# A two-layer graph kernel: attended half of the gate products in three f16 passes, products taken mask by mask, and a reordered first stage

## The chip, the cores and the metric

The kernel runs on one core of a Trainium2 chip. The metric is the device time of one execution in microseconds (us). The engines are TensorE (PE, with its weight loads shown as PEld), VectorE (DVE), ScalarE (ACT), GpSimd (POOL) and SyncE (SP), which issues most of the DMAs. Each engine works through its own list in order, and they meet only at semaphores.

## What is computed

There are 8192 nodes with 128 features each, and an adjacency matrix of 8192 x 8192 zeros and ones.

```python
h = relu(layernorm(x))
# first layer: graph attention, then a gated (GRU) update
Wh = h @ W;  src = Wh @ a[:F];  dst = Wh @ a[F:]
e = leaky_relu(src + dst.T, 0.2)
att = softmax(where(adj > 0, e, NEG_INF), axis=1)
h_prime = att @ Wh
gi = h_prime @ w_ih.T + b_ih          # the "attended half" of the gates
gh = h @ w_hh.T + b_hh
r = sigmoid(i_r + h_r);  z = sigmoid(i_z + h_z);  n = tanh(i_n + r * h_n)
x = x + (1 - z) * n + z * h
# second layer: plain aggregation
h = relu(layernorm(x))
x = x + adj @ (h @ W1.T + b1)
```

## The kernel before, in words

The file also has a path for any adjacency; it runs only where a check at the end asks for it, and takes no part here. The work is in `binary_adjacency`.

**First stage (0 to about 107 us).** Layernorm of all rows, their transposes, `h @ W` with its two attention columns (`column` and `features` on ACT, `weighted` on PE), and stores of h in two layouts. SP issues the stores in a loop over k = 0..15, and among them two loads of adjacency chunks (X, 2 MB each). Then come some small DVE operations on the attention columns and tables of f16 numbers (TB): `exp` factors times `Wh`, split into a high and a low half (`table_product`, `table_high`, `table_low`).

**Attention stage (107 to about 1139 us).** The rows are taken in 32 blocks of 256, called slots, g = 0..31. A slot has four chunks c = 0..3 of 2048 columns. For each chunk DVE and ACT make a mask "src + dst is positive" (`compare`, L669, 7 tiles on DVE; `sign_mask`, L468, 9 tiles on ACT), DVE turns the adjacency chunk into bytes (`ones_of`, L618), and combines both into two masks (`combine`: AND at L677, mask 1, and XOR at L681, mask 2). PE multiplies both masks with the tables: 64 matmuls of 259 columns for a chunk (`products`, L893), accumulating in four PSUM banks A[t][m], t being the half of the 256 rows and m the mask. ACT also counts the ones of each chunk (L477).

When the slot is done, its sums go through a tail that runs beside the next slots. With q = g - 1, in slot g: ACT copies the four banks (`evacuate`, L489), DVE forms `h_prime` in hp (`attended`, L686 to L702, placed after DVE's chunk c = 1), PE transposes it after its chunk 0 (L903, semaphore g_a), ACT copies the transpose to hpT (`attended_columns`, L503, semaphore g_1, placed in ACT's chunk 3), and PE computes the gates after its chunk 1 (`gates`, L916 to L919), preceded by a wait on g_1 and by the transposes of the normed rows of g - 2 (`normed`, L925). The sigmoids, tanh, update, second layernorm and the product with W1 (`projected`, L936) follow one or two slots later.

The chunk numbers of the engines are not the same time. DVE makes the masks of a slot while PE multiplies those of the slot before or the chunks just made: DVE's `attended` for slot g - 1 stands after DVE's chunk 1 of slot g, and it can start only when PE has ended slot g - 1.

**Second stage (1139 us to the end).** The mask bytes, stored by the first layer, are read again and multiplied with the projected rows (`span` and `rest`, L975).

The order on each engine is written out by hand in `slot`, `after` and `each_row_block` (slots 0 to 3 and the last two are written out, the rest is a loop over pairs). The lines that matter most here:

```python
def after(g, u, k, c):                 # PE, behind each chunk's products
    if c == 0 and in_range(g, 1):
        attended(g - 1)
    if c == 1:
        if in_range(g, 1):
            pe.wait_ge(g_1, g)
        if in_range(g, 2):
            normed(g - 2)
        if in_range(g, 1):
            gates(g - 1, 1 - u, k if u else k - 1)
```

Of the kernel before, what the change touches and what calls it, by code (L numbers as in the profile page):

```python
# [35 lines left out]
WNORM = 2.0  # L36
STEEP = 2.0 ** 60
# [30 lines left out]
def binary_adjacency(nc, sem, redo, xb, adjb, w, wt, a, wiht, whht, b_ih, b_hh, w1t, b1, out):  # L68
    ctx = ExitStack()
    with ctx:  # L70
# [18 lines left out]
        hpT = sb("hpT", [P, RW])  # L89
# [5 lines left out]
        wihT = sb("wihT", [P, 3 * F])  # L95
# [9 lines left out]
        rden = sb("rden", [P, 2])  # L105
# [12 lines left out]
        den = sb("den", [P, NT])  # L118
# [27 lines left out]
        dmb = rz[:, :, :].rearrange("p t f -> p (t f)")[:, 0:P]  # L146
# [18 lines left out]
        A = [[ps(f"A{t}{m}") for m in range(2)] for t in range(2)]  # L165
# [5 lines left out]
        WB = [A[0][0], A[0][1], A[1][0], A[1][1]]  # L171
        TP = [TG, GQ]
        PH2 = [A[0][0], A[0][1], A[1][0], A[1][1]]
# [12 lines left out]
        t_sc = k_w = sem("t_sc")  # L186

# [7 lines left out]
        e_t0, e_ev = sem("e_t0"), [sem(f"e_ev{t}") for t in range(2)]  # L195
# [40 lines left out]
        with nc.Block() as block:  # L236
            @block.sync
            def _(sp):
# [8 lines left out]
                for k in range(16):  # L247
# [105 lines left out]
            def _(pool):  # L353
# [21 lines left out]
                nc.gpsimd.tensor_tensor(brow[0:2, :], brow[0:2, :], bhid, ALU.add).then_inc(p_bias, 1)  # L375
                src = [brow] + bres
                for k in range(3):
                    pool.wait_ge(p_bias, 2 * k + 1)
                    nc.gpsimd.tensor_copy(bpart[k], src[k]).then_inc(p_bias, 1)
                    if k < 2:  # L380
                        pool.wait_ge(p_bias, 2 * k + 2)
                        nc.gpsimd.tensor_tensor(bres[k], src[k], bpart[k], ALU.subtract).then_inc(p_bias, 1)
                for q in range(4, 8):
                    deviation(q)
                pool.wait_ge(b_in, 112)
                nc.gpsimd.memset(TB[:, :, :, 2 * TW:2 * TW + 2], 1.0).then_inc(p_one, 1)

                def slot(g, u, k):
                    if in_range(g, 2):
                        q = g - 2  # L390
                        pool.wait_ge(d_ve, q + 1)
# [7 lines left out]
            def _(act):  # L399
# [4 lines left out]
                act.dma_start(wihT[:, :], wiht).then_inc(wt_in, 16)  # L404
# [8 lines left out]
                def features(k):  # L413
                    for b in range(2):
                        act.wait_ge(p_wh, 2 * k + b + 1)
                        t = k * 4 + b * 2
                        nc.scalar.activation(
                            WG[:, t:t + 2, 0:F + 2],
                            WB[(2 * k + b) % 4][:, 0:2 * (F + 2)].rearrange("p (t f) -> p t f", f=F + 2),
                            ACT.Copy).then_inc(p_ev, 1)  # L420
# [33 lines left out]
                def sign_mask(g, u, k, c):  # L454
# [8 lines left out]
                    for jj in range(first_on_act(g), JC):  # L463
                        if isinstance(g, int) and g == 0 and jj == JC // 2:
# [16 lines left out]
                def evacuate(q):  # L481
                    for t in range(2):
                        if t == 0:
                            act.wait_ge(e_t0, q + 1)
# [3 lines left out]
                        for m in range(2):  # L488
                            ins = nc.scalar.activation(AE[:, 2 * t + m, 0:2 * TW + 1], A[t][m][:, 0:2 * TW + 1], ACT.Copy)  # L489
                        ins.then_inc(e_ev[t], 1)  # L490

                def gate_sigmoids(q):
                    act.wait_ge(g_b, q + 1)
                    wait(act, d_x1, q)
                    nc.scalar.activation(rz[:, :, :], GP3[:, :, 0:2 * F], ACT.Sigmoid).then_inc(g_2, 1)

                def candidate(q):
                    act.wait_ge(d_tmp, q + 1)
                    nc.scalar.activation(nn[:, :, :], tmp[:, :, :], ACT.Tanh).then_inc(g_3, 1)
# [64 lines left out]
            def _(dve):  # L564
# [56 lines left out]
                ones_of(0, 0, 0, 0)  # L621
                dve.wait_ge(p_ev, 32)
# [17 lines left out]
                nc.vector.tensor_copy(srow, GP[0:NT, P:2 * P]).then_inc(p_sq, 1)  # L640

# [41 lines left out]
                def attended(q):  # L683
                    for t in range(2):
                        dve.wait_ge(e_ev[t], q + 1)
                    nc.vector.tensor_tensor(AE[:, :, 0:TW], AE[:, :, 0:TW], AE[:, :, TW:2 * TW], ALU.add).then_inc(d_sum, 1)  # L686
                    nc.vector.tensor_tensor(cn[:, bass.ts(q, 2)],
                                            AE[:, 0:4:2, 2 * TW:2 * TW + 1].rearrange("p t f -> p (t f)"),
                                            AE[:, 1:4:2, 2 * TW:2 * TW + 1].rearrange("p t f -> p (t f)"), ALU.add)
                    dve.wait_ge(d_sum, q + 1)  # L690
                    for t in range(2):
                        ins = nc.vector.scalar_tensor_tensor(nm[:, t, :], AE[:, 2 * t + 1, 0:TW],
                                                             ct[:, bass.ds(q * 2 + t, 1)], AE[:, 2 * t, 0:TW], ALU.mult,
# [4 lines left out]
                    nc.vector.reciprocal(rden[:, :], total).then_inc(d_rec, 1)  # L698
                    nc.vector.tensor_copy(den[:, bass.ts(q, 2)], total)
                    dve.wait_ge(d_rec, q + 1)  # L700
                    for t in range(2):
                        ins = nc.vector.tensor_scalar(hp[:, t * F:(t + 1) * F], nm[:, t, 0:F], rden[:, t:t + 1], None,  # L702
                                                      ALU.mult)
                    ins.then_inc(d_hp, 1)

# [7 lines left out]
                def updated(q, u, n):  # L713
# [23 lines left out]
                    dve.wait_ge(d_mv, q + 1)  # L737
                    nc.vector.tensor_scalar(ve[:, :], mv[:, :, 1:2].rearrange("p t k -> p (t k)"), EPS, None,  # L738
                                            ALU.add).then_inc(d_ve, 1)
# [14 lines left out]
                def slot(g, u, k):  # L754
                    main = in_range(g, 0)
                    first = isinstance(g, int) and g == 0
                    for c in range(CS):
                        if main:
# [12 lines left out]
                            combine(g, c)  # L771
                        if c == 0 and in_range(g, 2):
# [913 lines left out]
```

## Time and profile before

| what | value |
|---|---|
| median of 3 runs | 1602.78 us (1601.82 to 1603.23) |
| the profiled execution's own time | 1601.98 us |
| its span, first to last instruction | 1600.4 us |
| mean granted TensorE clock | 0.985 of 2.4 GHz |
| busy: PE | 1534.7 us (96%) |
| busy: DVE | 1125.8 us (70%), 193.6 us of each 200 us in the attention stage |
| busy: ACT | 1071.0 us (67%), 192.6 us of each 200 us in the attention stage |
| busy: POOL | 40.5 us (3%) |

The time lies 1.6 us above the span. The busy shares are means over stages: DVE and ACT are nearly full until 1107 us and nearly idle behind it, PE is full from 132 us on. In the timelines a matmul's duration includes its way through the array; the rate of the engine is read from start to start. One slot takes 32.76 us in the attention stage.

### The profile page before, as it was taken

What the parts mean: (1) busy time and instruction counts of PE and PEld (TensorE: products, weight loads), DVE (VectorE), ACT (ScalarE), POOL (GpSimd) and SP (SyncE); (2) the same over time, 40 slices, a digit from 0 to 9 for tenths busy, and PEclk for the clock granted to TensorE, in tenths of its full rate; (3) what the DMA queues carried; (4) which work ended last, traced back from release to release, by engine and by line L of the source; (5) the groups of instructions that cost most, each with busy time, mean ns of one, the idle gap of its engine ahead of it and who ended that gap; (6) DMA issues with size and microseconds to landing.
All of it is one profiled execution on the core that took longest, in us unless ns stands there. A gap on an engine that the chain in (4) does not pass through costs nothing.

```text
span 1600.4 us, 34919 instructions
## 1 busy us (share of the span) xinstructions
PE 1534.7 (96%) x13260; PEld 1333.3 (83%) x13260; DVE 1125.8 (70%) x2274; ACT 1071.0 (67%) x1820; POOL 40.5 (3%) x59
## 2 busy tenths in 40 slices
PE   6369999999999999999999999999999999999998
PEld 5257888888888888888888888888888888888887
DVE  7898999999999999999999999999250000000001
ACT  6689999999999999999999999999121000000000
POOL 4000000000000000000000000000000000000000
PEclk9779999999999999999999999999999999999999
DMA  8759899999999999999999998997468444444430
GB/s 306 292 217 358 332 342 340 345 339 337 342 342 344 332 342 343 342 343 332 340 341 334 346 344 333 346 345 265 191 242 334 177 176 163 156 161 170 177 126 15
DMA packets 79954, 454.15 MB, mean 284 GB/s; under 512 B 9176, under 2 KB 38434, under 8 KB 58914
## 3 DMA queue, kind: packets, MB, share of 16 engines
q1 hardware_dynamic: 78322, 444.54, 74.9%
q10 hardware_dynamic: 1584, 8.98, 1.4%
q8 instruction: 28, 0.46, 0.1%
q14 instruction: 20, 0.16, 0.0%
HBM read 369.57 MB, written 83.92 MB: 283 GB/s over the span
## 4 chain that ended last, share of the span: by engine, by line
PE 93%; DVE 4%; ACT 1%; issue 1%; DMA 1%; SPq 0%; DVEq 0%
PE A L893 56%; PE A L975 28%; PE GP L917 3%; PE GP L918 2%; PE GQ L936 1%; PE GP L919 1%; PE GP L916 1%; ACT M L468 1%; DVE Y L618 1%; DVE JK L568 1%; DMA X<-in_adjb_dram 1%; DVE M L585 0%; PE TG L903 0%; PE TG L925 0%; DVE M L681 0%
## 5 line engine op out<-in xcount | busy, mean ns | idle before, releaser
L893 PE MATMUL A<-TB,M 128*128 128x259 f16 x8192 | 942.4, 275 | 37.8 <-DVE M L681 31.9
L893 PEld LDWEIGHTS A<-TB,M 128*128 128x128 fp8e4 x8192 | 798.2, 97 | 165.4 <-issue 39.0
L468 ACT ACTIVATE M<-SB,dsteep 128x256 fp8e4<-128x256 f32 x1180 | 484.5, 504 | 0.0
L477 ACT ACTIVATE JK<-X 128x4096 uint8<-128x4096 uint32 x124 | 448.4, 3616 | 0.0
L618 DVE TENSOR_SCALAR Y<-X 128x4096 fp8e4<-128x4096 f32 x128 | 293.1, 2290 | 9.9 <-DMA X<-in_adjb_dram 9.6
L796 DVE SCALAR_TENSOR_TENSOR hp<-A,R 128x256 f32<-128x256 f32 x32 | 13.6, 425 | 367.5 <-PE A L975 348.2
L669 DVE TENSOR_SCALAR M<-SB,nd 128x256 fp8e4<-128x256 f32 x868 | 238.4, 349 | 0.0
L975 PE MATMUL A<-WG,X 128*128 128x256 f16 x2048 | 225.7, 273 | 0.0
L975 PE MATMUL A<-WG,TB 128*128 128x256 f16 x2048 | 225.2, 273 | 0.0
L975 PEld LDWEIGHTS A<-WG,TB 128*128 128x128 fp8e4 x2048 | 200.4, 98 | 23.2
L975 PEld LDWEIGHTS A<-WG,X 128*128 128x128 fp8e4 x2048 | 200.4, 98 | 23.1
L681 DVE TENSOR_TENSOR M<-Y,M 128x1024 uint32<-128x1024 uint32 x128 | 156.8, 1225 | 4.5
L677 DVE TENSOR_TENSOR M<-M,Y 128x1024 uint32<-128x1024 uint32 x128 | 156.3, 1221 | 0.5 <-issue 0.4
L489 ACT ACTIVATE AE<-A 128x259 f32<-128x259 f32 x128 | 42.0, 385 | 43.4 <-PE A L893 43.4
L917 PE MATMUL GP<-wihT,hpT 128*128 128x384 f32 x128 | 51.7, 486 | 0.0
L392 POOL TENSOR_TENSOR rstd<-ve,half 128x2 f32<-128x2 f32 x32 | 22.7, 709 | 1108.6 <-DVE ve L738 1108.6
L686 DVE TENSOR_TENSOR AE<-AE 128x516 f32<-128x516 f32 x32 | 22.4, 700 | 22.9 <-ACT AE L489 22.8
L918 PEld LDWEIGHTS GP<-whhT,R 128*128 128x128 f32 x128 | 24.3, 190 | 17.0
L918 PE MATMUL GP<-whhT,R 128*128 128x256 f32 x128 | 38.1, 379 | 0.0
L919 PEld LDWEIGHTS GP<-whhT,R 128*128 128x128 f32 x128 | 24.3, 190 | 3.3
L555 ACT ACTIVATE JK<-M 128x4096 uint8<-128x4096 uint32 x4 | 14.5, 3617 | 18.6 <-DMA M<-in_adjb_dram 18.6
L917 PEld LDWEIGHTS GP<-wihT,hpT 128*128 128x128 f32 x128 | 24.3, 190 | 2.4
(132 smaller groups left out, 687.3 us busy)
## 6 DMA issues: line engine op xcount, KB each, us to landing
X<-in_adjb_dram SPq DMA_DIRECT2D x128, 2048.0 KB, 9.2
mask_bytes<-Y SPq DMA_DIRECT2D x128, 512.0 KB, 4.8
X<-mask_bytes SPq DMA_DIRECT2D x16, 2048.0 KB, 9.3
TB<-mask_bytes SPq DMA_DIRECT2D x16, 2048.0 KB, 9.2
M<-in_adjb_dram ACTq DMA_DIRECT2D x4, 2048.0 KB, 10.6
M<-in_xb_dram SPq DMA_DIRECT2D x8, 512.0 KB, 8.4
h_rows<-M SPq DMA_DIRECT2D x8, 512.0 KB, 3.6
R<-in_xb_dram SPq DMA_DIRECT2D x32, 128.0 KB, 6.7
```

Of the source, the lines that this page charges most:

```text
L468: ins = nc.scalar.activation(rows(mask1(c), jj), SB[u][:, :], ACT.Sigmoid, scale=STEEP, bias=dsteep[:, j:j + 1], saturate=False)
L477: nc.scalar.activation(junk, X[c % 2][:, :].bitcast(u32), ACT.Sign, accum_out=nz[:, bass.ts(g, 1), c:c + 1].rearrange("p g c -> p (g c)")) ...
L489: ins = nc.scalar.activation(AE[:, 2 * t + m, 0:2 * TW + 1], A[t][m][:, 0:2 * TW + 1], ACT.Copy)
L618: nc.vector.tensor_scalar(Y[c % 2][:, :].bitcast(f8), X[c % 2][:, :], 1.0, MARK, ALU.is_equal, ALU.mult, saturate=False).then_inc(c_y, 1)
L669: ins = nc.vector.tensor_scalar(rows(mask1(c), jj), SB[u][:, :], nd[:, j:j + 1], None, ALU.is_ge, saturate=False)
L677: nc.vector.tensor_tensor(mask1(c), mask1(c), Y[c % 2][:, :], ALU.bitwise_and).then_inc(c_m1, 1)
L681: nc.vector.tensor_tensor(mask2(c), Y[c % 2][:, :], mask1(c), ALU.bitwise_xor).then_inc(c_m2, 1)
L893: ins = nc.tensor.matmul(A[t][m][:, 0:2 * TW + 1], rows((mask1, mask2)[m](c), jj)[:, t * P:(t + 1) * P], TB[:, c * JC + jj, m, 0:2 * TW + ...
L917: nc.tensor.matmul(bank[:, 0:3 * F], a_t, wihT[:, :], start=False, stop=False)
L918: nc.tensor.matmul(bank[:, 0:2 * F], h_t, whhT[:, 0:2 * F], start=False, stop=False)
L919: ins = nc.tensor.matmul(bank[:, 3 * F:4 * F], h_t, whhT[:, 2 * F:3 * F], start=False, stop=True)
L975: ins = nc.tensor.matmul(PH2[b][:, d * 2 * F:(d + 1) * 2 * F], YB[b][:, j * RW + d * P:j * RW + (d + 1) * P], GS[:, j, :], start=(d == 0 a ...
```

## The change: what it does

1. **Gate products.** hpT, the transposed `h_prime`, becomes a pair of f16 tiles: ACT writes the high half, and a new DVE operation `attended_low` writes the low half (transpose minus high half). The weights wihT become a pair of f16 tiles too, scaled by 64. PE replaces one f32 matmul of 384 columns by three f16 matmuls (high x high, high x low, low x high). PE's wait on g_1 (ACT's copy) becomes a wait on a_lo (DVE's low half; a_lo is the semaphore t_lo counted on). Biases and whhT are scaled by 64 on POOL, and the sigmoid and tanh scale back.
2. **Products mask by mask.** In each chunk PE takes the 32 matmuls of mask 1 for both halves of the rows, then the 32 of mask 2. The waits for the masks are split likewise.
3. **Merged copies.** The PSUM banks are laid out so that one ACT copy covers the two banks of a mask (`evacuate`) and the four blocks of `features`.
4. **First stage.** The load of the first X is issued at k = 9 instead of 11; DVE's first `ones_of` stands behind the small operations on the attention columns instead of ahead of them; ACT makes its second pair of table halves after 6 mask tiles instead of 8.
5. **Small moves.** The add of epsilon moves from DVE to POOL, a DVE copy (`den`, L699) goes, and the final check gets two more DVE operations.

```diff
-        hpT = sb("hpT", [P, RW])
+        hpT = sb("hpT", [P, 2, RW], f16)
-        wihT = sb("wihT", [P, 3 * F])
+        wihT = sb("wihT", [P, 2, 3 * F], f16)
-        A = [[ps(f"A{t}{m}") for m in range(2)] for t in range(2)]
+        ACC = ps("ACC", 4 * 512)
+        bank = [ACC[:, b * 512:(b + 1) * 512] for b in range(4)]
+        A = [[bank[2 * m + t] for m in range(2)] for t in range(2)]
+        a_lo = t_lo
@@ SP, first stage
-                    if k in (11, 15):
-                        b = k // 4 - 2
+                    if k in (9, 15):
+                        b = k // 15
                         sp.dma_start(X[b][:, :], adjb[b, :, :]).then_inc(c_in[b], 16)
@@ ACT
-                        if isinstance(g, int) and g == 0 and jj == JC // 2:
+                        if isinstance(g, int) and g == 0 and jj == JC // 2 - 2:
                 def evacuate(q):
-                    for t in range(2):
-                        if t == 0:
-                            act.wait_ge(e_t0, q + 1)
+                    for m in range(2):
+                        if m == 0:
+                            act.wait_ge(e_m0, q + 1)
                         else:
                             act.wait_ge(c_pe, (q + 1) * CS)
                         wait(act, d_hp, q)
-                        for m in range(2):
-                            ins = nc.scalar.activation(AE[:, 2 * t + m, 0:2 * TW + 1], A[t][m][:, 0:2 * TW + 1], ACT.Copy)
-                        ins.then_inc(e_ev[t], 1)
+                        nc.scalar.activation(AE[:, 2 * m:2 * m + 2, 0:2 * TW + 1], A3[m][:, :, 0:2 * TW + 1], ACT.Copy).then_inc(
+                            e_ev[m], 1)
-                    nc.scalar.activation(hpT[:, :], TG[:, 0:RW], ACT.Copy).then_inc(g_1, 1)
+                    nc.scalar.activation(hpT[:, 0, :], TG[:, 0:RW], ACT.Copy).then_inc(g_1, 1)
@@ DVE
-                ones_of(0, 0, 0, 0)
-                dve.wait_ge(p_ev, 32)
+                dve.wait_ge(p_ev, 16)
...
+                ones_of(0, 0, 0, 0)
-                    nc.vector.tensor_copy(den[:, bass.ts(q, 2)], total)
+                def attended_low(q):
+                    dve.wait_ge(g_1, q + 1)
+                    nc.vector.tensor_tensor(hpT[:, 1, :], TG[:, 0:RW], hpT[:, 0, :], ALU.subtract).then_inc(a_lo, 1)
...
                             combine(g, c)
+                        if c == 3 and in_range(g, 1):
+                            attended_low(g - 1)
@@ PE
-                def products(g, c, t):
-                    for jj in range(JC):
-                        for m in range(2):
+                def products(g, c, m):
+                    for t in range(2):
+                        for jj in range(JC):
                 def gates(q, u, n):
-                    pe.wait_ge(g_1, q + 1)
+                    pe.wait_ge(a_lo, 16 + q + 1)
...
-                        nc.tensor.matmul(bank[:, 0:3 * F], a_t, wihT[:, :], start=False, stop=False)
+                        for left, part in ((a_t, 0), (a_t, 1), (a_l, 0)):
+                            nc.tensor.matmul(bank[:, 0:3 * F], left, wihT[:, part, :], start=False, stop=False)
                     if c == 1:
                         if in_range(g, 1):
-                            pe.wait_ge(g_1, g)
+                            pe.wait_ge(a_lo, 16 + g)
-                        pe.wait_ge(c_m2, g * CS + c + 1)
-                        for t in range(2):
+                        for m in range(2):
+                            pe.wait_ge((c_m1, c_m2)[m], g * CS + c + 1)
                             if c == 0:
-                                wait(pe, e_ev[t], g)
+                                wait(pe, e_ev[m], g)
```

How the order changes on DVE, in slot 3: the masks of chunks 2 and 3, and what follows them. M is the mask tile, Y the adjacency bytes, h2n the normed rows. Before:

```order
L702 TENSOR_SCALAR hp<-nm,rden 128x128 x2
L669 TENSOR_SCALAR M<-SB,nd 128x256 x7
L618 TENSOR_SCALAR Y<-X 128x4096
L677 TENSOR_TENSOR M<-M,Y 128x1024
L681 TENSOR_TENSOR M<-Y,M 128x1024
L745 TENSOR_SCALAR h2n<-R,mv,rstd 128x128 x2
L751 SCALAR_TENSOR_TENSOR WG<-GQ,WG 128x2x128
L669 TENSOR_SCALAR M<-SB,nd 128x256 x7
L618 TENSOR_SCALAR Y<-X 128x4096
L677 TENSOR_TENSOR M<-M,Y 128x1024
L681 TENSOR_TENSOR M<-Y,M 128x1024
```

The same place on DVE after the change:

```order
L717 TENSOR_SCALAR hp<-nm,rden 128x128 x2
L685 TENSOR_SCALAR M<-SB,nd 128x256 x7
L634 TENSOR_SCALAR Y<-X 128x4096
L693 TENSOR_TENSOR M<-M,Y 128x1024
L697 TENSOR_TENSOR M<-Y,M 128x1024
L761 TENSOR_SCALAR h2n<-R,mv,rstd 128x128 x2
L767 SCALAR_TENSOR_TENSOR WG<-GQ,WG 128x2x128
L685 TENSOR_SCALAR M<-SB,nd 128x256 x7
L634 TENSOR_SCALAR Y<-X 128x4096
L693 TENSOR_TENSOR M<-M,Y 128x1024
L697 TENSOR_TENSOR M<-Y,M 128x1024
L723 TENSOR_TENSOR hpT<-TG,hpT 128x256
```

The new last row is `attended_low`. It stands behind both chunks' masks, two chunks behind the operation that made hp.

On PE, slot 2, from the transposes of hp (L903) to the gates, with the semaphores that an instruction waits for. Before:

```order
L903 MATMUL TG<-ident,hp 128x128
L893 MATMUL A<-TB,M 128x259 [waits c_m2]
L893 MATMUL A<-TB,M 128x259 x63
L925 MATMUL TG<-ident,h2n 128x128 [waits d_h2,g_1]
L925 MATMUL TG<-ident,h2n 128x128
L916 MATMUL GP<-BI,onesb 128x512 [waits d_tmp,g_in1,g_1]
L917 MATMUL GP<-wihT,hpT 128x384
L918 MATMUL GP<-whhT,R 128x256
L919 MATMUL GP<-whhT,R 128x128
```

The same place on PE after the change:

```order
L925 MATMUL TG<-ident,hp 128x128
L915 MATMUL ACC<-TB,M 128x259 [waits c_m1]
L915 MATMUL ACC<-TB,M 128x259 x31
L915 MATMUL ACC<-TB,M 128x259 [waits c_m2]
L915 MATMUL ACC<-TB,M 128x259 x31
L949 MATMUL TG<-ident,h2n 128x128 [waits d_h2,t_lo]
L949 MATMUL TG<-ident,h2n 128x128
L939 MATMUL GP<-BI,onesb 128x512 [waits d_tmp,g_in1,t_lo]
L941 MATMUL GP<-wihT,hpT 128x384 x3
L942 MATMUL GP<-whhT,R 128x256
L943 MATMUL GP<-whhT,R 128x128
```

The gate block stands at the same place. The semaphore it waits for has changed from g_1 (ACT) to t_lo (DVE's L723), and the f32 matmul with wihT is three f16 matmuls.

## Rows read from the trace of the kernel before

**Rows 1.** the page: busy times, and the chain that ended last by engine

```profile
PE 1534.7 (96%) x13260; PEld 1333.3 (83%) x13260; DVE 1125.8 (70%) x2274; ACT 1071.0 (67%) x1820; POOL 40.5 (3%) x59
...
PE 93%; DVE 4%; ACT 1%; issue 1%; DMA 1%; SPq 0%; DVEq 0%
```

**Rows 2.** timeline of PE, 500 to 535 us: start, us, engine, line, operation, count

```profile
509.87 14.48 PE L893 MATMUL A<-TB,M 128*128 128x259 f16 x128
...
524.40 7.32 PE L893 MATMUL A<-TB,M 128*128 128x259 f16 x64
531.56 0.38 PE L925 MATMUL TG<-ident,h2n 128*128 128x128 f32 x2
531.78 0.38 PE L916 MATMUL GP<-BI,onesb 128*128 128x512 bf16 x1
532.00 0.81 PE L917 MATMUL GP<-wihT,hpT 128*128 128x384 f32 x2
532.64 0.59 PE L918 MATMUL GP<-whhT,R 128*128 128x256 f32 x2
...
534.81 0.39 PE L893 MATMUL A<-TB,M 128*128 128x259 f16 x2
```

**Rows 3.** waits, 200 to 1100 us: total, times, longest

```profile
DVE AE L686 <- ACT AE L489: 13.2, 25, 0.7
```

**Rows 4.** timeline of DVE, 500 to 535 us

```profile
507.91 0.42 DVE L711 TENSOR_TENSOR tmp<-tmp,GP 128x256 f32<-128x256 f32 x1
...
517.99 0.70 DVE L686 TENSOR_TENSOR AE<-AE 128x516 f32<-128x516 f32 x1 [0.56 <-ACT AE L489]
...
519.57 0.17 DVE L699 COPY den<-nm 128x2 f32 x1
519.67 0.48 DVE L702 TENSOR_SCALAR hp<-nm,rden 128x128 f32<-128x128 f32 x2
...
529.19 2.29 DVE L618 TENSOR_SCALAR Y<-X 128x4096 fp8e4<-128x4096 f32 x1
531.39 1.22 DVE L677 TENSOR_TENSOR M<-M,Y 128x1024 uint32<-128x1024 uint32 x1
...
533.79 1.40 DVE L669 TENSOR_SCALAR M<-SB,nd 128x256 fp8e4<-128x256 f32 x5
```

**Rows 5.** timeline of ACT, 500 to 535 us

```profile
517.23 0.66 ACT L489 ACTIVATE AE<-A 128x259 f32<-128x259 f32 x2 [1.23 <-PE A L893]
...
528.55 0.37 ACT L503 ACTIVATE hpT<-TG 128x256 f32<-128x256 f32 x1
```

**Rows 6.** timeline of DVE and PE, 75 to 150 us

```profile
78.56 8.94 PE L893 MATMUL A<-TB,M 128*128 128x259 f16 x64 [5.09 <-DVE M L681]
...
106.34 1.23 DVE L681 TENSOR_TENSOR M<-Y,M 128x1024 uint32<-128x1024 uint32 x1
...
107.67 9.72 PE L893 MATMUL A<-TB,M 128*128 128x259 f16 x64 [4.40 <-DVE M L681]
...
138.71 1.92 DVE L669 TENSOR_SCALAR M<-SB,nd 128x256 fp8e4<-128x256 f32 x7
...
139.28 0.38 PE L916 MATMUL GP<-BI,onesb 128*128 128x512 bf16 x1
```

**Rows 7.** PE in two stretches: us, busy (count), granted clock, DMA share, GB/s

```profile
78.00:80.00 2.00, 1.44 (x7) 0.63 1.08 303
118.00:120.00 2.00, 0.00 (x0) 0.87 0.95 352
```

**Rows 8.** timeline of SP, ACT and DVE, first stage

```profile
34.96 0.45 SPq L255 DMA_DIRECT2D X<-in_adjb_dram  x1
...
41.67 0.83 ACT L417 ACTIVATE WG<-A 128x260 f32<-128x260 f32 x2 [0.20 <-PE A L866]
...
44.23 2.29 DVE L618 TENSOR_SCALAR Y<-X 128x4096 fp8e4<-128x4096 f32 x1 [7.18 <-DMA X<-in_adjb_dram]
...
49.20 1.23 DVE L654 TENSOR_TENSOR AE<-WG,bt 128x1032 f32<-128x1032 f32 x1
```

More of the change, by code:

```diff
@@ L36 @@
 WNORM = 2.0
+WSCALE = 64.0
+WMOST = 2.0 ** 28
 STEEP = 2.0 ** 60
@@ L163, in binary_adjacency @@
         x1_d = nc.dram_tensor("x_after_gat", [P, NT, F], f32).ap()
-        A = [[ps(f"A{t}{m}") for m in range(2)] for t in range(2)]
+        ACC = ps("ACC", 4 * 512)
+        bank = [ACC[:, b * 512:(b + 1) * 512] for b in range(4)]
+        A = [[bank[2 * m + t] for m in range(2)] for t in range(2)]
+        A3 = [ACC[:, m * 1024:(m + 1) * 1024].rearrange("p (t f) -> p t f", f=512) for m in range(2)]
         TG = ps("TG")
@@ L194, in binary_adjacency @@
         g_in = [sem(f"g_in{b}") for b in range(2)]
-        e_t0, e_ev = sem("e_t0"), [sem(f"e_ev{t}") for t in range(2)]
+        e_m0, e_ev = sem("e_m0"), [sem(f"e_ev{m}") for m in range(2)]
         d_sum, d_n, d_rec, d_hp = sem("d_sum"), sem("d_n"), sem("d_rec"), sem("d_hp")
@@ L384, in _ @@
                     deviation(q)
+                pool.wait_ge(wt_in, 48)
+                nc.gpsimd.tensor_scalar(wihf, wihf, WSCALE, None, ALU.mult).then_inc(p_bias, 1)
+                nc.gpsimd.tensor_scalar(whhT[:, :], whhT[:, :], WSCALE, None, ALU.mult).then_inc(p_bias, 1)
+                pool.wait_ge(p_bias, 8)
+                nc.gpsimd.tensor_copy(wihT[:, 0, :], wihf).then_inc(p_bias, 1)
+                pool.wait_ge(p_bias, 10)
+                nc.gpsimd.tensor_tensor(wihT[:, 1, :], wihf, wihT[:, 0, :], ALU.subtract).then_inc(p_bias, 1)
                 pool.wait_ge(b_in, 112)
@@ L390, in slot @@
                         q = g - 2
+                        pool.wait_ge(d_mv, q + 1)
+                        nc.gpsimd.tensor_tensor(ve[:, :], mv[:, :, 1:2].rearrange("p t k -> p (t k)"),
+                                                epst[:, 0:1].to_broadcast([P, 2]), ALU.add).then_inc(d_ve, 1)
                         pool.wait_ge(d_ve, q + 1)
@@ L413, in features @@
                 def features(k):
[L414 to L420, printed above, removed]
+                    act.wait_ge(p_wh, k + 1)
+                    nc.scalar.activation(
+                        WG[:, k * 4:k * 4 + 4, 0:F + 2].rearrange("p (b t) f -> p b t f", t=2),
+                        A3[k % 2][:, :, 0:2 * (F + 2)].rearrange("p b (t f) -> p b t f", f=F + 2),
+                        ACT.Copy).then_inc(p_ev, 1)
                 act.wait_ge(p_one, 1)
@@ L860, in weighted @@
                     pe.wait_ge(p_ht, k + 1)
+                    wait(pe, p_ev, k - 1)
                     for b in range(2):
-                        wait(pe, p_ev, 2 * k + b - 3)
                         for d in range(2):
@@ L914, in gates @@
                         bank = GP[:, t * 512:(t + 1) * 512]
-                        a_t, h_t = hpT[:, t * F:(t + 1) * F], HT[u][:, t * F:(t + 1) * F]
+                        a_t, a_l = [hpT[:, part, t * F:(t + 1) * F] for part in range(2)]
+                        h_t = HT[u][:, t * F:(t + 1) * F]
                         nc.tensor.matmul(bank, onesb[:, :], BI[:, 0:4 * F], start=True, stop=False)
-                        nc.tensor.matmul(bank[:, 0:3 * F], a_t, wihT[:, :], start=False, stop=False)
+                        for left, part in ((a_t, 0), (a_t, 1), (a_l, 0)):
+                            nc.tensor.matmul(bank[:, 0:3 * F], left, wihT[:, part, :], start=False, stop=False)
                         nc.tensor.matmul(bank[:, 0:2 * F], h_t, whhT[:, 0:2 * F], start=False, stop=False)
@@ L958, in slot @@
                                 pe.wait_ge(p_one, 3)
[L959 to L960 removed]
+                        for m in range(2):
+                            pe.wait_ge((c_m1, c_m2)[m], g * CS + c + 1)
                             if c == 0:
[L962 removed]
+                                wait(pe, e_ev[m], g)
                             pe.sem_inc(turn, 1)
[L964 to L965 removed]
+                            ins = products(g, c, m)
+                            if m == 1:
                                 ins.then_inc(c_pe, 1)
                             elif c == CS - 1:
[L968 removed]
+                                ins.then_inc(e_m0, 1)
                         after(g, u, k, c)
```

65 lines of the change are left out of this document (33 added, 32 removed).

## The prediction

> **What bounds the kernel now.** I read the page first, then the timelines of one slot in the middle, engine by engine, then the waits, then the first stage and the stretches in which the clock changes. The page says PE: it is busy 96% of the span and 93% of the chain that ended last lies on it [rows 1]. The timeline of PE shows no gap in a slot: 64 matmuls take 7.16 us (524.40 to 531.56), and the transposes and gate products behind them (531.56 to 534.81) and the next matmuls follow start to start [rows 2]. But DVE is not far behind. It waits for PE once in a slot, ahead of `attended` (L686), for only 0.53 us on average (13.2 us over 25 waits) [rows 3]. That wait ties the two engines together. PE ends a slot's products at about 517.03 (the second 64 of the 128 that start at 509.87 begin there a new slot) [rows 2], ACT copies the last banks from 517.23 [rows 5], and DVE starts `attended` at 517.99 [rows 4]. Everything that DVE does behind `attended` is thus fixed in time against the end of a PE slot, however fast PE becomes.
>
> **The new wait, the largest term.** Before, PE's gates waited for ACT's copy, which starts at 528.55 and takes 0.37 us [rows 5]; PE asks for it at 531.56, 2.6 us later [rows 2], so it costs nothing. Now they wait for `attended_low` on DVE. By the order it stands behind the masks of chunk 3, where in the timeline the next slot's `compare` starts: 533.79 [rows 4]. I take off 0.10 us for the copy L699 that goes (519.57 to 519.67) and add the operation itself, 256 elements from PSUM, like L711: 0.42 us [rows 4]. From the end of a DVE operation to PE's first matmul it is 0.10 us (106.34 + 1.23 to 107.67) [rows 6]. So PE goes on at 533.79 - 0.10 + 0.42 + 0.10 = 534.21 instead of 531.56: a gap of 2.65 us. Queued behind the waiting instruction on PE are `normed`, the gates and chunks 2 and 3, and DVE's next `attended` waits for the end of these. The loop closes: end of PE's slot, `attended`, two chunks of masks and the low half on DVE, gates, chunks 2 and 3 on PE. PE's earlier chunks are no part of it, so nothing that is saved there shortens it. Neither ACT nor the DMAs enter: ACT's copy is ready 5 us before DVE comes to it, and ACT and SP gain time in each slot. ACT may now have to wait for its sigmoids, but inside the slack that ACT gains ahead of its last evacuation (it waits 1.23 us there now [rows 5], and gets the 2.65 on top).
>
> **The three f16 passes.** The f32 matmul of 384 columns takes 0.64 us (532.00 to 532.64), the bf16 one of 512 columns 0.22 (531.78 to 532.00) [rows 2]. Three passes of 384 columns at that rate take 3 x 384 x 0.22 / 512 = 0.495 us. Two halves of the rows save 2 x 0.145 = 0.29 us a slot. This lies behind the gap and counts in full. Bounds: nothing (if the added weight loads show) to 0.33 us (if the products come a little under that rate).
>
> **Slot by slot.** Net 2.65 - 0.29 = 2.36 us. It holds in slots 2 to 30, 29 of them: 68.4 us (slot 2 has one DVE operation fewer; I leave that). In slot 1 DVE is early: 138.71 - 0.10 + 0.42 + 0.10 = 139.13, while PE's gates start at 139.28 [rows 6]: no gap, and 0.29 saved. In slot 31 DVE makes no bytes for a next slot, 2.20 us less (529.19 to 531.39 [rows 4]), so the gap is 0.45 and the net +0.16. The gates of slot 31, after the last slot, save 0.29; matmuls of the second stage cover their wait. Sum: 68.4 - 0.29 + 0.16 - 0.29 = 68.0 us.
>
> **The clock.** A gap in PE's work has a second price here. In the gap that begins at 107.67 + 9.72 = 117.39 [rows 6] the mean granted clock of 118 to 120 us is 0.87 [rows 7]; between full and half (2.4 and 1.2 GHz) this means that it fell at about 119.5, 2.1 us after the last matmul. In the gap of 5.09 us ahead of 78.56 it fell only at about 78.5 (0.63 over 78 to 80) [rows 6, 7]. So the delay varies from 2.1 to 5 us, as if against a beat that the kernel doesn't set, and a gap of 2.65 us lies within it. The smallest price on the page of the attention stage is that of the stretch at 78.56: 64 matmuls took 8.94 us against 7.32 at the full clock [rows 2, 6], 1.62 us more. All of PE's work behind the gap is on the loop, so this adds in full. With no fall the price is 0, with one in each of the 29 slots 47 us. The period of the slots has no reason to keep step with such a beat, so I take somewhat over half, 16 falls: 26 us. The Trainium skill ("TensorE: Matmul & The Clock Gate", section "HAM oscillation — how this bites in real kernels") names idle gaps between bursts of matmuls as what brings the low clock back, and counts a gap as short as the one foreseen here among the harmless; by it there would be no fall and the sum would end at 1670 us. The fall 2.1 us into a gap speaks against it.
>
> **Mask by mask.** PE can start a chunk one XOR (1.23 us, L681 [rows 6]) earlier. In the middle the masks are made many microseconds ahead of PE, so nothing comes of it. In slot 0, where PE waits for DVE, the last chunk starts 1.2 us earlier; but then PE waits from 117.39 to 123.31 for the banks of slot 0, which ACT copies only when its own list comes to it. The gain is swallowed: 0. The merged copies save less than 0.1 us behind the end of a slot; 0.
>
> **First stage.** DVE stands idle 7.18 us until the first X lands, and starts the tables at 49.20 [rows 8]. With X loaded earlier and the small operations first, these can start when `features` ends, 41.67 + 0.83 = 42.50 [rows 8]. With the scalings they last 2.7 us (from 44.23 + 2.29 to 49.20 [rows 8]), and `ones_of` adds 2.2: the tables at 47.4, 1.8 us earlier at best. Against it, X now lies in the queue ahead of stores of h for which ACT's last columns wait. The load takes from 34.96 to 44.23 [rows 8]; issued some 4 us earlier it lands at about 40, and stores behind it later still, which would delay the last columns by about 2 us. I take 0, with -1.8 and +1 as bounds. The six tiles instead of eight move ACT's work behind the second tables; ACT then ends its 16 tiles just as DVE wants them, so the chunk keeps its length. POOL's scaling of the weights is over long before 139 us, where the first gates need it, and its add of epsilon comes at the end of DVE's chunk 1, a whole chunk of masks before DVE wants the result. The two more operations of the final check lie where DVE waits for PE: 0.
>
> **Sum.** The profiled execution took 1601.98 us, 0.8 below the median shown. 1602.0 + 68.0 + 26 = 1696 us.
>
> **Rivals.**
> - *The gap comes, the clock holds*: 1602.0 + 68.0 = 1670 us. For it: the fall ahead of 78.56 needed 5 us. Against it: the one at 119.5.
> - *The clock falls in every slot*: 1602 + 68 + 47 = 1717 us, and up to some more if the low clock lasts longer than at 78.56 (64 matmuls took 9.72 at 107.67 [rows 6]).
> - *Faster*: the low half is there when PE asks, and only the shorter gates count. 31 slots and the last gates at 0.29 are 9 us: 1593 us. It decides at 531.56: DVE must have ended `attended_low` 2.65 us earlier than I place it. DVE's work up to there is fixed by the end of PE's slot and has no idle time but the wait at L686, so I see no way to it, unless the order in which DVE runs isn't the one written.
> - *No change*: the gap is only about 0.3 us, and the two terms cancel, for which the same would have to be off by 2.4 us.
>
> **How the numbers follow.** The forecast (gap, and falls in a part of the slots) has 0.57, with its own range 1684 to 1708. Clock holds 0.24, every slot or worse 0.10, faster 0.06, no change 0.01, and 0.02 for slower by less than 1660 us. The range reaches down to the case with the clock held less its bounds (the first stage's 1.8, a gap shorter by 0.1 us over 29 slots), 1665, and up to the case of a fall in each slot, 1717. Faster or slower means by over 0.2%, 3.2 us, about what a measurement of this kernel can tell from no change. Slower holds 0.57 + 0.24 + 0.10 + 0.02 = 0.93.
>
> **What would show it.** In the profile after: PE idle about 2.6 us in each slot ahead of the transposes of h2n, released by DVE's subtraction into hpT; `attended` waiting for ACT's copy some 3 us instead of 0.5; a slot of about 35.1 us, and of 36.7 where the clock fell; DVE and ACT busy some 7% less of the attention stage; wihT's three matmuls about 0.165 us apart; the granted clock at one half behind a part of the gaps. Wrong would be: a slot of 32.5 us with no wait for hpT (then the place of `attended_low` in time is wrong), a slot of 35.1 throughout (then the clock held), or a first stage off by over 2 us.

## The result, and the profile after

| | before | after |
|---|---|---|
| median of the runs | 1602.63 us (1601.82 to 1603.23, 4 runs) | 1697.2 us (1696.48 to 1698.31, 4 runs) |
| ratio to before, 95% interval | | 1.059 (1.0576 to 1.0603) |
| span of the profiled execution | 1600.4 us | 1696.1 us |
| mean granted TensorE clock | 0.985 | 0.970 |

The change made the kernel 94.6 us slower. The forecast was 1696 us.

The page of the changed kernel, busy times and the chain by engine. PE was at 96% and 93% of the chain [rows 1]:

```profile
PE 1550.1 (91%) x13324; PEld 1348.6 (80%) x13324; DVE 1132.2 (67%) x2245; ACT 1073.2 (63%) x1740; POOL 50.7 (3%) x96
...
PE 63%; DVE 18%; issue 12%; ACT 4%; DVEq 1%; DMA 1%; SPq 0%; ACTq 0%
```

PE still does nearly the same work, but it is no longer alone on the chain: DVE has 18% of it, and "issue" 12%. The large pieces of "issue" are DVE's too: in the slot shown below the chain has one of 1.97 us at 529.39, while DVE's L634 runs (529.16 to 531.44). Who waits for whom is told by the waits from 200 to 1200 us (engine and line, what it waited for, us in total, times, longest):

```profile
PE TG L949 <- DVE hpT L723: 76.0, 28, 2.8
DVE AE L702 <- ACT AE L505: 74.6, 27, 2.9
...
ACT rz L511 <- PE GP L943: 59.3, 28, 2.9
PEld TG L949 <- issue: 42.4, 14, 3.1
PEld TG L949 <- DVE hpT L723: 41.4, 14, 3.0
```

L949 are the transposes of h2n that follow the wait for a_lo, L723 is the new `attended_low`. PE waits there 28 times for 76 us in this stretch. Of the weight loads (PEld) that start the block, half are put down to "issue" and half to L723, by 3 us each. DVE in turn now waits 2.8 us (74.6 us over 27 times) for the end of PE's slot, where it had waited 0.53 [rows 3].

A slot near the one in [rows 2] (there it is slot 13, here slot 12), PE from 505 to 538 us:

```profile
509.88 14.35 PE L915 MATMUL ACC<-TB,M 128*128 128x259 f16 x128
...
524.28 7.26 PE L915 MATMUL ACC<-TB,M 128*128 128x259 f16 x64
534.30 0.43 PE L949 MATMUL TG<-ident,h2n 128*128 128x128 f32 x2 [2.76 <-DVE hpT L723]
534.57 0.38 PE L939 MATMUL GP<-BI,onesb 128*128 128x512 bf16 x1
534.78 0.65 PE L941 MATMUL GP<-wihT,hpT 128*128 128x384 f16 x3
535.27 0.59 PE L942 MATMUL GP<-whhT,R 128*128 128x256 f32 x2
...
537.28 2.93 PE L915 MATMUL ACC<-TB,M 128*128 128x259 f16 x25
```

The 64 matmuls end at about 531.4, and PE goes on at 534.30. The three f16 matmuls take 0.49 us (534.78 to 535.27), against 0.64 for the f32 one. DVE beside it, with `attended`, the chunk 3 and the low half:

```profile
517.88 0.70 DVE L702 TENSOR_TENSOR AE<-AE 128x516 f32<-128x516 f32 x1 [2.80 <-ACT AE L505]
...
529.16 2.28 DVE L634 TENSOR_SCALAR Y<-X 128x4096 fp8e4<-128x4096 f32 x1
531.36 1.21 DVE L693 TENSOR_TENSOR M<-M,Y 128x1024 uint32<-128x1024 uint32 x1
532.61 1.22 DVE L697 TENSOR_TENSOR M<-Y,M 128x1024 uint32<-128x1024 uint32 x1
533.75 0.42 DVE L723 TENSOR_TENSOR hpT<-TG,hpT 128x256 f16<-128x256 f32 x1
534.09 1.92 DVE L685 TENSOR_SCALAR M<-SB,nd 128x256 fp8e4<-128x256 f32 x7
```

L723 starts at 533.75 and ends at 534.17; PE's first matmul comes 0.13 us later. That these times lie within 0.1 us of those in the forecast (533.69 and 534.21) is chance, since it is another slot. What can be compared is the distance from the start of `attended`: 15.87 us to L723 (forecast 533.69 - 517.99 = 15.70) and 16.42 us to PE (forecast 16.22). ACT's copy had been ready since 528.45 + 0.36:

```profile
514.38 0.59 ACT L505 ACTIVATE AE<-ACC 128x518 f32<-128x518 f32 x1
517.17 0.60 ACT L505 ACTIVATE AE<-ACC 128x518 f32<-128x518 f32 x1 [2.20 <-PE ACC L915]
...
528.45 0.36 ACT L519 ACTIVATE hpT<-TG 128x256 f16<-128x256 f32 x1
...
537.48 0.60 ACT L511 ACTIVATE rz<-GP 128x512 f32<-128x512 f32 x1 [1.21 <-PE GP L943]
```

The last row shows ACT waiting 1.21 us for the gates; its wait ahead of the second copy at 517.17 grew from 1.23 to 2.20 us, so nothing of this reached the end of the slot.

**Where the 95 us are.** From one group of hp transposes on PE to the next (before L903, after L925) is one slot. Read from the timelines of PE:

```
                    first group  last group  the slots between (us)
before              131.91       1145.86     31.9; 29 x 32.76 or 32.77; 31.9
after               133.82       1241.87     31.31; 34.57; 34.91; 11 x about 35.1; 16 x 36.66 to 36.86; 32.07
```

The 31 slots grew by 94.1 us, the part ahead of the first group by 1.9, and the part behind the last one shrank by 0.3. There are two lengths of a slot, 35.1 and 36.8 us. They mostly alternate, and four times two long ones follow each other. What the longer ones have is the clock. PE in stretches of 2 us behind the gap of the slot before the one shown (us, busy, count, granted clock, DMA share, GB/s):

```profile
494.00:496.00 2.00, 0.77 (x7) 1.00 0.81 342
496.00:498.00 2.00, 0.54 (x4) 1.00 1.06 322
498.00:500.00 2.00, 2.00 (x9) 0.61 0.97 344
500.00:502.00 2.00, 2.00 (x7) 0.54 0.96 410
502.00:504.00 2.00, 2.00 (x20) 1.00 0.91 365
```

and the block in it:

```profile
497.46 0.44 PE L949 MATMUL TG<-ident,h2n 128*128 128x128 f32 x2 [2.69 <-DVE hpT L723]
...
497.94 0.68 PE L941 MATMUL GP<-wihT,hpT 128*128 128x384 f16 x3
498.43 1.05 PE L942 MATMUL GP<-whhT,R 128*128 128x256 f32 x2
499.27 0.63 PE L943 MATMUL GP<-whhT,R 128*128 128x128 f32 x2
```

The gap ended at 497.46 after 2.69 us. The clock was still at its full level until then and fell at about 498.4, when PE was at work again: what follows the first three f16 passes takes up to twice as long (L942 to L943 0.84 us instead of 0.43). It was at its lower level of 1.2 GHz (0.54 over 500 to 502) and back at about 501.8. The slot shown in full above had no fall.

### The profile page after: what moved, and what is told of

It is laid out like the page before. It is cut to its first block, busy times and chain, and to the rows that moved or that the text cites. A ratio compares the mean times of both kernels' runs of the same rounds, so it can differ in the third digit from the quotient of the medians.

```text
span 1696.1 us, 35030 instructions
## 1 busy us (share of the span) xinstructions
PE 1550.1 (91%) x13324; PEld 1348.6 (80%) x13324; DVE 1132.2 (67%) x2245; ACT 1073.2 (63%) x1740; POOL 50.7 (3%) x96
## 4 chain that ended last, share of the span: by engine, by line
PE 63%; DVE 18%; issue 12%; ACT 4%; DVEq 1%; DMA 1%; SPq 0%; ACTq 0%
PE ACC L915 27%; PE ACC L999 26%; DVE M L685 6%; DVE M L693 4%; PE GP L941 2%; ACT M L485 2%; PE GP L942 2%; PE GP L943 1%; PE GQ L960 1%; PE GP L939 1%; ACT AE L505 1%; ACT JK L494 1%; PE TG L949 1%; DVE hpT L723 1%; DVE h2n L761 1%
## 5 line engine op out<-in xcount | busy, mean ns | idle before, releaser
L915 PE MATMUL ACC<-TB,M 128*128 128x259 f16 x8192 | 934.6, 276 | 41.3 <-DVE M L693 32.7
L915 PEld LDWEIGHTS ACC<-TB,M 128*128 128x128 fp8e4 x8192 | 806.2, 98 | 153.8 <-issue 42.5
L634 DVE TENSOR_SCALAR Y<-X 128x4096 fp8e4<-128x4096 f32 x128 | 292.4, 2285 | 2.3 <-DMA X<-in_adjb_dram 2.2
L999 PE MATMUL ACC<-WG,X 128*128 128x256 f16 x2048 | 225.7, 273 | 0.0
L999 PE MATMUL ACC<-WG,TB 128*128 128x256 f16 x2048 | 225.2, 273 | 0.0
L999 PEld LDWEIGHTS ACC<-WG,TB 128*128 128x128 fp8e4 x2048 | 200.4, 98 | 23.2
L999 PEld LDWEIGHTS ACC<-WG,X 128*128 128x128 fp8e4 x2048 | 200.4, 98 | 23.1
L693 DVE TENSOR_TENSOR M<-M,Y 128x1024 uint32<-128x1024 uint32 x128 | 155.9, 1218 | 26.8 <-ACT M L485 24.5
L697 DVE TENSOR_TENSOR M<-Y,M 128x1024 uint32<-128x1024 uint32 x128 | 156.8, 1225 | 4.4
L949 PE MATMUL TG<-ident,h2n 128*128 128x128 f32 x64 | 13.8, 298 | 78.6 <-DVE hpT L723 78.6
L505 ACT ACTIVATE AE<-ACC 128x518 f32<-128x518 f32 x64 | 38.1, 596 | 72.1 <-PE ACC L915 72.1
L702 DVE TENSOR_TENSOR AE<-AE 128x516 f32<-128x516 f32 x32 | 22.3, 698 | 88.4 <-ACT AE L505 88.4
L949 PEld LDWEIGHTS TG<-ident,h2n 128*128 128x128 f32 x64 | 6.5, 140 | 87.0 <-DVE hpT L723 44.6
L511 ACT ACTIVATE rz<-GP 128x512 f32<-128x512 f32 x32 | 19.1, 597 | 66.2 <-PE GP L943 66.2
L941 PE MATMUL GP<-wihT,hpT 128*128 128x384 f16 x192 | 52.3, 391 | 0.0
L942 PE MATMUL GP<-whhT,R 128*128 128x256 f32 x128 | 48.2, 466 | 0.0
L941 PEld LDWEIGHTS GP<-wihT,hpT 128*128 128x128 f16 x192 | 21.7, 113 | 17.6 <-issue 7.8
```

Source lines behind the costliest of these rows:

```text
L505: nc.scalar.activation(AE[:, 2 * m:2 * m + 2, 0:2 * TW + 1], A3[m][:, :, 0:2 * TW + 1], ACT.Copy).then_inc(e_ev[m], 1)
L634: nc.vector.tensor_scalar(Y[c % 2][:, :].bitcast(f8), X[c % 2][:, :], 1.0, MARK, ALU.is_equal, ALU.mult, saturate=False).then_inc(c_y, 1)
L693: nc.vector.tensor_tensor(mask1(c), mask1(c), Y[c % 2][:, :], ALU.bitwise_and).then_inc(c_m1, 1)
L697: nc.vector.tensor_tensor(mask2(c), Y[c % 2][:, :], mask1(c), ALU.bitwise_xor).then_inc(c_m2, 1)
L915: ins = nc.tensor.matmul(A[t][m][:, 0:2 * TW + 1], rows((mask1, mask2)[m](c), jj)[:, t * P:(t + 1) * P], TB[:, c * JC + jj, m, 0:2 * TW + ...
L941: nc.tensor.matmul(bank[:, 0:3 * F], left, wihT[:, part, :], start=False, stop=False)
```

## The experiments

All eight were timed in three rounds against the kernel before. The short names are those of the runs. Slot times are read from the timelines of PE as above.

**e1_low_early: the low half ahead of the adjacency bytes.**

```diff
                                 compare(g, u, k, c)
+                            if c == 3 and in_range(g, 1):
+                                attended_low(g - 1)
                             if c < CS - 1:
...
-                        if c == 3 and in_range(g, 1):
+                        if c == 3 and not main and in_range(g, 1):
                             attended_low(g - 1)
```

(`main` holds in slots 0 to 31; only behind them is the old place kept.)

> The changed kernel with one instruction moved: DVE makes the low half right behind the compare of chunk 3 (where ACT's copy is just ready), ahead of the adjacency bytes and the two combines, some 4.5 us earlier. My theory (the loss is PE's wait for this instruction): the gap of 2.9 us ahead of the transposes of h2n goes, the clock stays at its full level, and a slot takes 32.2 to 32.4 us, set by the shorter gates on PE or by DVE, which has 0.5 us of slack and gets 0.1 more work; 1586 to 1594 us. Rival (the loss lies in the f16 products or the new product order themselves, or in DVE's added work): the time stays above 1650 us.

Measured 1586.81 us (1586.47 to 1587.65), ratio 0.9907 (0.9891 to 0.9924): moving this one instruction ahead of three others on DVE (L634, L693 and L697) is worth 110 us. PE in this run:

```profile
519.06 7.26 PE L917 MATMUL ACC<-TB,M 128*128 128x259 f16 x64
526.15 0.38 PE L951 MATMUL TG<-ident,h2n 128*128 128x128 f32 x2
...
526.59 0.65 PE L943 MATMUL GP<-wihT,hpT 128*128 128x384 f16 x3
```

No gap at 526.15. Slots take 32.19 us until about 620 us and then 32.22 and 32.37 in turn. DVE shows why:

```profile
513.68 0.25 DVE L754 BATCH_NORM_AGGREGATE mv<-st 128x2 f32<-128x6 f32 x2
513.85 0.67 DVE L702 TENSOR_TENSOR AE<-AE 128x516 f32<-128x516 f32 x1
...
525.11 0.41 DVE L723 TENSOR_TENSOR hpT<-TG,hpT 128x256 f16<-128x256 f32 x1
```

`attended` (L702) follows the operation before it with no wait, and L723 stands at 525.11. DVE's slack of 0.5 us is gone, and it sets the slot by now and then. That the loss lies in the f16 products or in DVE's added work is excluded.

**e2_f32_gates: the change without its f16 part.** One f32 product with wihT, no low half, PE waits for ACT's copy; all else stays changed.

```diff
-                    pe.wait_ge(a_lo, 16 + q + 1)
+                    pe.wait_ge(g_1, q + 1)
...
-                        for left, part in ((a_t, 0), (a_t, 1), (a_l, 0)):
-                            nc.tensor.matmul(bank[:, 0:3 * F], left, wihT[:, part, :], start=False, stop=False)
+                        nc.tensor.matmul(bank[:, 0:3 * F], a_t, wihT[:, :], start=False, stop=False)
```

> The changed kernel without its first part: one f32 product with wihT instead of three f16 ones, no low half on DVE, PE waits for ACT's copy as before; product order, merged copies and first stage stay changed. My theory: everything but the low half is harmless: no gap, slots of 32.5 us (products in the new order came 110.9 ns apart instead of 111.9), 1592 to 1600 us. Rival (the mask-by-mask order or the first stage has a part in the loss): above 1610 us.

Measured 1595.0 us (1594.52 to 1596.84), ratio 0.9959 (0.9945 to 0.9973). Slots take 32.50 us. All parts of the change but the low half's place are harmless or help. Between e2 and e1 lies the f16 part without its wait: 32.50 - 32.19 = 0.31 us a slot while PE sets the pace (forecast 0.29), 8 us in all.

**e3_wait_alone: the kernel before, with nothing but the wait.**

```diff
+                def attended_low(q):
+                    dve.wait_ge(g_1, q + 1)
+                    nc.vector.tensor_tensor(lowT[:, :], TG[:, 0:RW], hpT[:, :], ALU.subtract).then_inc(t_lo, 1)
...
+                        if c == 3 and in_range(g, 1):
+                            attended_low(g - 1)
...
-                            pe.wait_ge(g_1, g)
+                            pe.wait_ge(t_lo, 16 + g)
```

> The kernel before with the suspected wait alone: DVE makes a low half into a tile that nothing reads, at the place where the change has it, and PE's gates (still f32) wait for it. My theory: 30 gaps of about 2.7 us (80 us) and about 17 falls of the clock at 1.65 us (28 us): 1700 to 1718 us. Rival (the wait costs only part of the 95 us, the rest is in the f16 products): 1640 to 1680 us.

Measured 1723.37 us (1722.96 to 1723.91), ratio 1.0759 (1.0741 to 1.0777). The wait alone costs more than the whole change. The gap is as expected; its block, where the clock then fell (PE):

```profile
504.94 0.44 PE L932 MATMUL TG<-ident,h2n 128*128 128x128 f32 x2 [2.53 <-DVE lowT L709]
505.21 0.52 PE L923 MATMUL GP<-BI,onesb 128*128 128x512 bf16 x1
505.53 1.49 PE L924 MATMUL GP<-wihT,hpT 128*128 128x384 f32 x2
506.81 1.06 PE L925 MATMUL GP<-whhT,R 128*128 128x256 f32 x2
...
542.21 0.44 PE L932 MATMUL TG<-ident,h2n 128*128 128x128 f32 x2 [2.61 <-DVE lowT L709]
```

What I had wrong is the number of falls. Slots without one take 35.5 us and those with one 37.2; I count 24 falls in the 29 full slots, not 17. The gap is a little shorter than in the changed kernel (2.5 to 2.6 us against 2.7), so a longer gap is not the reason. The traces show when the falls come. PE in two stretches of 1 us, in the block above and in the one behind the gap at 542.21:

```profile
505.00:506.00 1.00, 1.00 (x4) 0.66 0.84 147
542.00:543.00 1.00, 0.79 (x4) 0.93 0.73 152
```

Between full and half these means put the falls at 505.32 and 542.86: 0.4 and 0.65 us behind PE's return, and 37.5 us apart. Of the 23 distances between falls in e3, 18 are 37.5 us and the other 5 are 71.7. The slots take 37.2, so each fall comes about 0.3 us later behind PE's return than the last, and after one at 1.1 to 1.4 us a slot is passed over. In the changed kernel 11 of the 15 distances are 71.7 us and 4 are 37.5; a slot without a fall and one with it take 71.9 together, so there it is mostly every second slot. The falls thus keep a time that the slots don't set, and the length of the slots decides how many of them meet it. What sets that time no run shows.

**e4_filled_gap: matmuls in the gap.**

```diff
+                            wait(pe, d_lo, g - 2)
+                            for _ in range(0 if isinstance(g, int) and g >= NS else 12):
+                                nc.tensor.matmul(GQ[:, 0:512], TBf[:, 0:P], TBf[:, 0:512], start=True, stop=True,
+                                                 skip_group_check=True)
                             pe.wait_ge(a_lo, 16 + g)
```

> The changed kernel with 12 matmuls of 512 columns more in each slot, written to a bank that nobody reads then, just ahead of the wait for the low half: PE works through most of the gap (12 x 0.215 = 2.6 us of 2.9) and waits for the rest. The end of the gap does not move. My theory (slots of 36.8 instead of 35.1 us are those behind whose gap the clock fell): all slots take 35.1 us, the granted clock stays at 1.00 from 200 us on, 17 x 1.7 = 29 us less: 1664 to 1672 us. Rival (the longer slots have another cause, or the clock falls for another reason than idle time): 1690 to 1700 us.

Measured 1676.21 us (1675.96 to 1676.94), ratio 1.0466 (1.0448 to 1.0483). More work on PE made the kernel 21 us faster. Slots 4 to 29 take 35.09 to 35.18 us, and the granted clock of 200 to 1000 us is 1.00. PE's gap and its stretch of 400 us:

```profile
526.60 2.75 PE L971 MATMUL GQ<-TB 128*128 128x512 f16 x12
529.53 0.43 PE L949 MATMUL TG<-ident,h2n 128*128 128x128 f32 x2 [0.18 <-DVE hpT L723]
```

```profile
400.00:600.00 200.00, 199.16 (x1678) 1.00 0.88 318
600.00:800.00 200.00, 199.34 (x1683) 1.00 0.88 317
```

It ended 4 to 12 us above what I expected. The matmuls cost 2.6 us in slot 1 (33.90 instead of 31.31) and 1.9 in slot 31 (34.01 instead of 32.07), where there was little or no gap to fill; I had left that out, and with it 16 falls at 1.7 us, 27 us, agree with the gain.

**e5_swapped_loops: the product order alone, in the kernel before.**

```diff
-                    for jj in range(JC):
-                        for m in range(2):
+                    for m in range(2):
+                        for jj in range(JC):
```

> The kernel before with only two inner loops of the products swapped: within each half of the rows first the 16 matmuls of mask 1, then the 16 of mask 2, so that 16 matmuls in a row write the same bank instead of alternating between two. If the order of the banks sets the rate (my reading of 110.9 ns instead of 111.9 between matmuls in the changed kernel), slots take 32.5 us and the whole 1593 to 1596 us. Rival (the rate comes from the new layout of the banks or from the earlier wait for mask 1): no change, 1601 to 1604 us.

Measured 1594.49 us (1593.28 to 1596.91), ratio 0.9949 (0.9932 to 0.9966). Slots take 32.50 us, 0.26 us less than before, 1.0 ns for each of 256 matmuls. So it is the order of the loops, and neither the layout of the banks nor the split wait. The order changes two things at once: 16 matmuls in a row write one bank, where two banks took turns, and the tiles that are read (of the two masks, and of the two parts of the tables) no longer take turns either. Which of the two gives the 1.0 ns no run parts.

**e8_low_middle: the low half between the bytes and the combine.**

```diff
                                 ones_of(g + 1, 1 - u, k + u, 0)
+                            if c == 3 and in_range(g, 1):
+                                attended_low(g - 1)
                             combine(g, c)
```

> The changed kernel with the low half made between the adjacency bytes and the combine of chunk 3: 2.4 us earlier than in the change, 2.3 us later than in the run with it behind the compare. If each microsecond that DVE comes later is one on PE, a gap of 0.4 to 0.6 us is left in each slot, slots take 32.6 to 32.9 us, the clock doesn't fall, and the time is 1599 to 1608 us. Rival (it is the wait as such, or the clock falls at small gaps too): above 1620 us.

Measured 1600.84 us (1599.69 to 1602.25), ratio 0.9991 (0.9981 to 1.0). PE waits 0.3 us:

```profile
524.20 7.26 PE L917 MATMUL ACC<-TB,M 128*128 128x259 f16 x64
531.79 0.44 PE L951 MATMUL TG<-ident,h2n 128*128 128x128 f32 x2 [0.33 <-DVE hpT L723]
```

and DVE in the same slot:

```profile
517.80 0.73 DVE L702 TENSOR_TENSOR AE<-AE 128x516 f32<-128x516 f32 x1 [0.36 <-ACT AE L505]
...
531.32 0.41 DVE L723 TENSOR_TENSOR hpT<-TG,hpT 128x256 f16<-128x256 f32 x1
```

Slots take 32.7 to 32.8 us, and no slot is lengthened by the clock. The three places of one instruction on DVE give 32.2 to 32.4, 32.75 and 35.1 us: from the middle place to the last it comes 2.35 us later (13.52 and 15.87 us behind the start of `attended`) and the slot is 2.35 us longer. From the first to the middle place most of the way is free.

**e6_x_at_11: as e1, with the first X at k = 11 again.**

```diff
-                    if k in (9, 15):
-                        b = k // 15
+                    if k in (11, 15):
+                        b = k // 15
```

> The kernel with the low half behind the compare, and the first load of X issued at k = 11 again, as before; the rest of the new first stage stays. If the load at k = 9 held up the stores that ACT's last columns wait for (1.7 us in the changed kernel), ACT's features end near 42.6 us, the tables start at 47.4 us instead of 49.4, and the time is 2 us less than with k = 9: 1584 to 1586 us. Rival (the start is swallowed by the later waits of slot 0 and 1): 1586 to 1588 us.

Measured 1583.99 us (1583.36 to 1584.88), ratio 0.9886 (0.9869 to 0.9902), against 1586.81 of e1, which ran beside other runs of the kernel before. The intervals of the two (e1: 0.9891 to 0.9924) overlap a little, so it is the traces that show what the place of the load does. The first stage of the changed kernel, ACT and DVE:

```profile
41.36 0.60 ACT L430 ACTIVATE Y<-TG 128x512 f32<-128x512 f32 x1 [1.71 <-DMA h_columns<-Y]
...
44.19 0.60 ACT L434 ACTIVATE WG<-ACC 128x520 f32<-128x520 f32 x1 [0.38 <-PE ACC L888]
...
49.42 1.23 DVE L670 TENSOR_TENSOR AE<-WG,bt 128x1032 f32<-128x1032 f32 x1
```

The columns of h wait 1.71 us for a store, which lies behind X in the queue. With k = 11 that wait is gone:

```profile
40.19 0.60 ACT L430 ACTIVATE Y<-GQ 128x512 f32<-128x512 f32 x1
...
42.04 0.60 ACT L434 ACTIVATE WG<-ACC 128x520 f32<-128x520 f32 x1 [0.37 <-PE ACC L890]
...
47.27 1.23 DVE L670 TENSOR_TENSOR AE<-WG,bt 128x1032 f32<-128x1032 f32 x1
```

The tables start 2.15 us earlier, and PE's slot 1 at 121.68 instead of 123.84.

**e7_evac_early: as e6, and in slot 1 ACT copies the banks before it counts.**

```diff
+                        if c == 1 and isinstance(g, int) and g == 1:
+                            evacuate(g - 1)
                         if main:
                             if c + 1 < EARLY:
...
-                        if c == 1 and in_range(g, 1):
+                        if c == 1 and in_range(g, 1) and not (isinstance(g, int) and g == 1):
                             evacuate(g - 1)
```

> As the run with X at k = 11, and in slot 1 alone ACT copies the banks of slot 0 ahead of its count of chunk 2 instead of behind it (3.6 us earlier). PE waits for these copies from 115 to 124 us in the changed kernel. If ACT's order sets that wait, PE starts slot 1 some 3.6 us earlier, of which DVE, which waited 2.1 us for the same copies and has no slack left, lets 2 to 3.6 through: 1581 to 1583 us. Rival (DVE's masks or the load of X hold slot 1 back): 1584 to 1586 us.

Measured 1582.19 us (1582.02 to 1583.17), ratio 0.9876 (0.986 to 0.9893). PE starts slot 1 3.4 us earlier (118.32 instead of 121.68), but only 2.0 us arrive at the end of the attention stage: DVE, which is full now, gained only its own wait of 2.1 us. Its interval touches that of e6 (0.9869 to 0.9902), so 1.8 us is the difference of the medians and no more. It is the fastest version run, 20 us below the kernel before and 115 below the changed one.

## Why the prediction was right, point by point

- *The new wait.* Right in place, size and mechanism. The end of the slot ties DVE's work down, and the low half comes 2.7 to 2.9 us too late. e3 shows that the wait alone does it, e1 that it goes with the place of one instruction, e8 that between the last two places each microsecond on DVE is one on PE. The net of a slot without a fall was forecast as 2.36 us and is 35.13 - 32.76 = 2.37. That is so partly by compensation. Counted from 531.4, the gap is 2.9 us, nearly 0.3 more than the 2.65 forecast. Of this 0.13 is only the faster products ahead of it. The other 0.14 is a longer way over DVE: from `attended` to L723 it is 0.17 us more than forecast, since the 0.10 us taken off for the copy L699 was not saved (`hp` starts 1.77 us behind `attended`, 1.68 before). PE's answer took 0.13 us, not 0.10, and `attended` itself came 0.06 us sooner behind the end of the slot. The faster products behind the gap, at 0.13 us, hid it.
- *The three f16 passes.* Forecast 0.29 us a slot, measured 0.31 between e2 and e1.
- *The clock.* Forecast 16 falls of 29 at 1.62 us, 26 us; measured 16 at 1.7 us, 27 us. e4 shows by taking the idle time away that the falls are its effect. The mechanism is shown, but the number was hit by luck: e3 with almost the same gap has 24. "The period of the slots has no reason to keep step" was wrong, too: the falls come every 71.7 or 37.5 us, and the slots, lengthened by the falls themselves, nearly keep step with that (71.9 us for two here, 37.2 for one in e3). The rival with the clock held (1670 us) is out. The rule of the Trainium skill ("TensorE: Matmul & The Clock Gate", section "HAM oscillation — how this bites in real kernels"), by which such a gap would have been harmless, does not hold here: the clock fell behind 16 gaps of 2.6 to 2.8 us.
- *Mask by mask.* "Nothing comes of it" was wrong in one respect. I weighed only the earlier start, not the rate. The order is worth 1.0 ns a matmul, 8 us where PE sets the pace (e5). In the changed kernel only the chunks behind the gap profit, 0.13 us a slot, which the longer way over DVE cancelled.
- *First stage.* Forecast 0, between -1.8 and +1. The tables started 0.22 us later and PE's slot 1 0.53 us later; the clock in its first chunk made it 1.9 us (10.14 instead of 8.76 us for the 64 matmuls). That lies outside the bounds; the clock in this chunk was no term of the forecast. The two opposed terms were right: e6 has the tables at 47.27 (best case 47.4), and the queue took back what the order gave.
- *Slots 1 and 31, the final check, POOL.* No gap in slot 1, 0.42 us in 31 (forecast 0.45), nothing behind the last slot.

What stays open: what sets the time that the falls keep, and why a fall comes up to 1.4 us behind PE's return and not later. The runs show that the number of falls isn't set by the gap's length alone.

## What to carry to other kernels

When a wait is moved from one engine to another, look up where in its list the new producer stands and what ties that list to the waiting engine. Here DVE had the mask work of two chunks between `attended` and the new instruction, and the instruction could be moved ahead of three others for free. In a loop closed through two engines a saving on the part outside the loop is worth nothing. A gap in PE had a second price here in the clock of the work behind it, so a gap that can't be closed may be worth filling.

## What the runs showed of the hardware that I had not expected

- The granted clock fell from 2.4 to 1.2 GHz behind gaps of 2.1 to 2.8 us in 16 of 29 slots (changed kernel) and 24 of 29 (e3, the shortest of them in slot 2), not during the gap but between PE's return and 1.4 us after it (497.46 and 498.4 in the slot shown). It did not fall behind gaps of 0.3 to 0.4 us (e8). Each fall cost 1.7 us.
- The falls lie 37.5 or 71.7 us apart in both kernels, whatever the length of the slots.
- 259-column matmuls with fp8 weights come 110.9 ns apart when 16 in a row take one mask, one part of the tables and one PSUM bank, and 111.9 ns apart when they alternate between two of each (e5).
- With a DMA of 2 MB issued 4 us earlier, ACT waited 1.71 us for a store behind it in the same queue; with the load in its old place (e6) it did not wait.
